# A token, attention and expert tower: value products on whole-number rows, and w1's split and sequence 0's work in other places

## The reference, cut

```python
# token layer: ids in 0..27; counts over a window of three tokens
fused = concat([emb[ids], window_mean(pca_lookup[ids]) @ proj_w + proj_b]) @ fus_w + fus_b
h = ln(fused, 1e-5) * ln_g + ln_b
# attention, 16 heads of 64
y0 = ln(h, 1e-5)
q, k, v = y0 @ Wq + bq, y0 @ Wk + bk, y0 @ Wv + bv
attn = softmax(q k^T / 8)
y = y0 + (attn v) @ Wo + bo
h = h + (ln(y, 1e-3) * gamma + beta)
# experts: 16, two per token, each takes the 64 tokens of a sequence with the greatest route
x = ln(h, 1e-5)
h = h + ln(x + experts(x), 1e-5) * gamma2 + beta2
```

## Time and profile before

| | us |
|---|---|
| median of three runs | 557.83 |
| lowest and highest | 548.49, 558.05 |
| the profiled execution | 547.54 |
| its span, first to last instruction | 545.7 |
| mean granted TensorE clock | 0.993 of full |

### The profile page before, as it was taken

The page is one execution under the profiler, slowest core; times in us unless marked ns, Lnnn a source line. Parts: engine busy times, 40 slices in busy tenths (PEclk is TensorE's granted clock), DMA queues, the critical chain, the costliest instruction groups (busy, mean ns, idle before and its releaser), DMA issues. The chain is left out here.

```text
span 545.7 us, 16180 instructions
## 1 busy us (share of the span) xinstructions
PE 508.7 (93%) x6079; PEld 378.7 (69%) x6079; DVE 439.1 (80%) x986; ACT 363.3 (67%) x766; POOL 379.3 (70%) x508
## 2 busy tenths in 40 slices
PE   5988869999999999999999999788999999999984
PEld 3876557777777777777777786643467767777664
DVE  4797558888888888988888888968777998887675
ACT  2667867878787877878787877517666565556530
POOL 1005567878787878878787878842268798788883
PEclk9998999999999999999999999999999999999998
DMA  7800000000000000000000000000733054261011
GB/s 235 322 4 2 2 2 3 3 3 4 3 2 3 4 2 3 3 3 4 3 2 4 4 2 3 2 0 2 165 82 88 23 131 97 61 145 46 29 40 59
DMA packets 11905, 21.74 MB, mean 40 GB/s; under 512 B 4668, under 2 KB 9780, under 8 KB 10164
## 3 DMA queue, kind: packets, MB, share of 16 engines
q1 hardware_dynamic: 11410, 20.15, 13.5%
q10 hardware_dynamic: 418, 0.55, 0.3%
HBM read 16.24 MB, written 4.33 MB: 38 GB/s over the span
## 5 line engine op out<-in xcount | busy, mean ns | idle before, releaser
L817 POOL TENSOR_TENSOR s_pl<-s_pf,s_ph 128x512 f16<-128x512 f32 x128 | 146.9, 1159 | 5.8 <-ACT s_ph L916 5.8
L1010 DVE TENSOR_REDUCE s_mx<-ps 128x4 f16<-128x512 f32 x128 | 83.8, 677 | 31.8 <-PE ps L1153 31.8
L795 PE MATMUL ps<-s_xt_all,s_w1s 128*128 128x512 f16 x384 | 87.9, 379 | 2.2 <-ACT s_ub L1467 1.6
L1622 PE MATMUL ps<-s_w2s,s_hid 128*128 128x256 f16 x768 | 88.9, 273 | 0.0
L910 ACT ACTIVATE s_pf<-ps 128x512 f32<-128x512 f32 x128 | 76.6, 602 | 15.6 <-PE ps L1166 15.5
L1622 PEld LDWEIGHTS ps<-s_w2s,s_hid 128*128 128x128 f16 x768 | 75.1, 98 | 11.0
L916 ACT ACTIVATE s_ph<-s_pf 128x512 f16<-128x512 f32 x128 | 77.2, 636 | 0.0
L1201 PE MATMUL ps<-s_zh,s_cth 128*128 128x256 f16 x256 | 69.8, 273 | 0.0
L1201 PE MATMUL ps<-s_zh,s_ctl 128*128 128x256 f16 x256 | 69.8, 273 | 0.0
L1201 PE MATMUL ps<-s_zl,s_cth 128*128 128x256 f16 x256 | 69.8, 273 | 0.0
L795 PEld LDWEIGHTS ps<-s_xt_all,s_w1s 128*128 128x128 f16 x384 | 37.3, 98 | 41.4 <-ACT s_ub L1467 2.1
(11 more groups left out here) (233 smaller groups left out, 1211.4 us busy)
## 6 DMA issues: line engine op xcount, KB each, us to landing
s_rep<-picks SPq DMA_DIRECT2D x14, 512.0 KB, 6.2
s_stage<-in_w SPq DMA_DIRECT2D x2, 1024.0 KB, 14.1
out<-s_ot_a SPq DMA_DIRECT2D x16, 128.0 KB, 1.7
out<-s_lg SPq DMA_DIRECT2D x16, 128.0 KB, 1.7
s_stage<-in_wq SPq DMA_DIRECT2D x1, 1024.0 KB, 5.0
s_stage<-in_wk SPq DMA_DIRECT2D x1, 1024.0 KB, 6.6
...
```

The lines of the kernel that those rows point to most:

```text
L795: mm = nc.tensor.matmul(hidden_bank(n)[:], w1s[:, wp, c, j * P:(j + 1) * P], xt_all[:, GB * g:GB * (g + 1), xp, c, :], start=(k == 0), sto ...
L817: nc.gpsimd.tensor_tensor(flat(pl[:, b % 2, 4 * j:4 * j + 4, :]), pf[:, j, :], flat(ph[:, b % 2, 4 * j:4 * j + 4, :]), ALU.subtract).then_ ...
L1010: nc.vector.tensor_reduce(mx[:, b % 2, c:c + 4], A[ab][:].rearrange("p (h k) -> p h k", h=4), AX.X, ALU.max).then_inc(max_done[hf][ab], 1)
L1622: mm = nc.tensor.matmul(zb[b % 4], hid[:, g % 2, hp, j, t * P:(t + 1) * P], w2s[:, wp, j, :], start=False, stop=(j == NJ - 1 and hp == 1))
```

## The change

- **Value products.** The exponentials get a bias per key token (partition), `ln_r`, the logarithm of `r12` times 0.25. So the probabilities hold the factor of `u`, and the value products can use `n` itself, in float16: `nk`, 56 whole numbers, which float16 holds without a low part. Column R2 and R2+1 hold `s1 = v1 * r1` as high and low part, ONE_HI and the next `s12 = s1 * s2`. A head takes two products of 60 columns. ScalarE converts `nb` into `nk` in the first stage, POOL makes the four columns there. The value table gets its R2 and its bias columns twice.
- **The sums** now are two columns: VectorE adds them (`sums`, a reduction of 128x16 to 128x8) and takes the reciprocal of the result from SBUF. The reduction stands where the reciprocal stood; the reciprocal follows the second reduction of maxima (half 0) and y_scaled (half 1). VectorE's waits on itself share one semaphore.
- **The logarithm** is computed once, for all sequences: ScalarE loads the Ln table in step -4, takes Ln of r12, loads Exp in step -3, takes exp(-ln); VectorE corrects it with two small operations (`log_rho`) in step -4 of its order, and the first two exps of sequence 0 wait for it.
- **The maxima** are float32, and `maxima_cols` a float32 transpose.
- **w1**: POOL makes its high part and scales in place before its loop; the low part is made in four pieces of 512 columns in steps -2 and -1, behind probs_lo.
- **Order at the start**: maxima_cols(0) stands ahead of the q products of sequence 1, score_cols(0, 0) ahead of token rows 11 to 13; both halves' first probs_hi of sequence 0 follow its exps directly; token row 13 goes to VectorE.
- `ot_a` lies in zh's place instead of a buffer of its own.

```diff
@@ -40,7 +40,8 @@
 R2, ONE, SHIFT = 2 * V, 2 * V + 1, 2 * V + 2
-UV = ONE + 1
+ONE_HI, UV = R2 + 2, R2 + 4
+RHO_SCALE = 0.25
@@ -118,7 +119,8 @@
 uh, ul = sb("uh", [P, 2, B, UD], F16), sb("ul", [P, 2, B, UD], F16)
-u_top, u_rest = uh[:, 0], ul[:, 0]
+u_top, u_rest, nk = uh[:, 0], ul[:, 0], uh[:, 1]
+r12, ln_r = sb("r12", [P, B]), sb("ln_r", [P, B])
@@ -262,6 +265,23 @@
         nc.gpsimd.memset(nb[:, :, R2:R2 + 1], 1.0).then_inc(cleared, 1)
+        pool.wait_ge(root_step, R1_STEP)
+        nc.gpsimd.tensor_tensor(s1[:], v1[:], r1[:], ALU.mult).then_inc(nk_step, 1)
+        pool.wait_ge(root_step, R2_STEP)
+        pool.wait_ge(v_ok, 1)
+        nc.gpsimd.tensor_tensor(s2[:], v2[:], r2[:], ALU.mult).then_inc(nk_step, 1)
+        pool.wait_ge(nk_step, 2)
+        nc.gpsimd.tensor_tensor(s12[:], s1[:], s2[:], ALU.mult).then_inc(nk_step, 1)
+        def column(n):
+            return nk[:, :, n:n + 1].rearrange("p b o -> p (b o)")
+        pool.wait_ge(nk_step, 3)
+        for n, src in ((R2, s1), (ONE_HI, s12)):
+            nc.gpsimd.tensor_scalar(column(n), src[:], 1.0, 0.0, ALU.mult, ALU.add).then_inc(nk_step, 1)
+        pool.wait_ge(nk_step, 5)
+        for n, src in ((R2, s1), (ONE_HI, s12)):
+            nc.gpsimd.tensor_tensor(column(n + 1), src[:], column(n), ALU.subtract)
@@ -280,6 +300,8 @@
                 .then_inc(nt_ok, 1)
+        act.wait_ge(n_ok, 2)
+        nc.scalar.activation(nk[:, :, 0:2 * V], nb[:, :, 0:2 * V], ACT.Copy)
@@ -302,8 +324,13 @@
             act.wait_ge(qkv_ok, 2 * n + 1)
-            nc.scalar.activation(qkv_t[:, n, :, ONE:ONE + 1], bT[:, n, :].rearrange("p (c o) -> p c o", o=1), ACT.Copy)\
-                .then_inc(qkv_ok, 1)
+            if n < 2:
+                nc.scalar.activation(qkv_t[:, n, :, ONE:ONE + 1], bT[:, n, :].rearrange("p (c o) -> p c o", o=1), ACT.Copy)\
+                    .then_inc(qkv_ok, 1)
+            else:
+                nc.scalar.activation(qkv_t[:, n, :, R2 + 1:R2 + 2], qkv_t[:, n, :, R2:R2 + 1], ACT.Copy).then_inc(qkv_ok, 1)
+                nc.scalar.activation(qkv_t[:, n, :, ONE_HI:UV], bT[:, n, :].rearrange("p (c o) -> p c o", o=1)
+                                     .to_broadcast([P, HD, 2]), ACT.Copy).then_inc(qkv_ok, 1)
@@ -633,7 +660,7 @@
                 pe.wait_ge(wo_step, 2 * HD + 1)
-                pe.wait_ge(qkv_ok, 6)
+                pe.wait_ge(qkv_ok, 7)
@@ -731,9 +758,10 @@
 ph, pl = sb2("ph", [P, 2, H, P], F16), sb2("pl", [P, 2, H, P], F16)
-mx = sb2("mx", [P, 2, H], F16)
+mx = sb2("mx", [P, 2, H])
 mrow = sb2("mrow", [H, 2, P], F16)
-rsum = sb2("rsum", [P, 2, 8])
+rsum, total = sb2("rsum", [P, 2, 8]), sb2("total", [P, 2, 8])
+ln_0, rho_x, rho_t = sb2("ln_0", [P, B]), sb2("rho_x", [P, B]), sb2("rho_t", [P, B])
@@ -853,6 +881,14 @@
                                     ALU.add, ALU.mult).then_inc(x_done, 1)
+        W1_PARTS = {(-2, 0): (0,), (-2, 1): (1,), (-1, 0): (2,), (-1, 1): (3,)}
+        def w1_lo(n):
+            part = slice(512 * n, 512 * n + 512)
+            if n == 0:
+                pool.wait_ge(w_hi, 12)
+            nc.gpsimd.tensor_tensor(both(w1s[:, 1])[:, part], stage2[:, 0, part], both(w1s[:, 0])[:, part], ALU.subtract)
@@ -873,8 +909,9 @@
         pool.wait_ge(w_hi, 10)
-        pool.wait_ge(w1_top, 1)
-        scale_and_lo(both(w1s[:, 0]), both(w1s[:, 1]), stage2[:, 0, :], 10)
+        nc.gpsimd.tensor_scalar(both(w1s[:, 0]), stage2[:, 0, :], W_SCALE, 0.0, ALU.mult, ALU.add).then_inc(w_hi, 1)
+        pool.wait_ge(w_hi, 11)
+        nc.gpsimd.tensor_scalar(stage2[:, 0, :], stage2[:, 0, :], W_SCALE, 0.0, ALU.mult, ALU.add).then_inc(w_hi, 1)
@@ -885,12 +922,16 @@
                 probs_lo(i + 2, 1)
+            for n in W1_PARTS.get((i, 0), ()):
+                w1_lo(n)
...
                 probs_lo(i + 2, 2)
+            for n in W1_PARTS.get((i, 1), ()):
+                w1_lo(n)
@@ -907,7 +948,9 @@
                 act.wait_ge(plo_done[j], b)
-            nc.scalar.activation(pf[:, j, :], ST[j % 2][:], ACT.Exp).then_inc(exp_done[j], 1)
+            if b == 0 and j < 2:
+                act.wait_ge(ln_ok, 4)
+            nc.scalar.activation(pf[:, j, :], ST[j % 2][:], ACT.Exp, bias=ln_r[:, b:b + 1]).then_inc(exp_done[j], 1)
@@ -948,26 +991,32 @@
-        ACT_TOKENS = {(-4, 0): (0, 1, 3, 4, 6, 7), (-3, 0): (9, 10), (-3, 1): (12, 13, 15)}
+        ACT_TOKENS = {(-4, 0): (0, 1), (-4, 2): (3, 4, 6, 7), (-3, 0): (9, 10), (-3, 1): (12, 15)}
...
                 context_hi(i + 1, 0)
-            if has(i + 2):
+            if has(i + 2) and i > -2:
                 probs_hi(i + 2, 1)
+            if i == -3:
+                max_row(0)
...
                 q_hi(i + 4, 0)
-            if has(i + 3):
+            if i == -3:
+                nc.scalar.preload_act_table(ACT.Exp)
+                act.wait_ge(ln_ok, 1)
+                nc.scalar.activation(rho_x[:], ln_0[:], ACT.Exp, scale=-1.0).then_inc(ln_ok, 1)
+            elif has(i + 3):
...
                 q_hi(i + 4, 1)
-            if i == -3:
-                nc.scalar.preload_act_table(ACT.Exp)
...
                 token_rows(n)
-            if i == -3:
-                act.wait_ge(in_w12, 48)
-                nc.scalar.activation(both(w1s[:, 0]), stage2[:, 0, :], ACT.Copy, scale=W_SCALE).then_inc(w1_top, 1)
+            if i == -4:
+                nc.scalar.preload_act_table(ACT.Ln)
+                nc.scalar.activation(ln_0[:], r12[:], ACT.Ln).then_inc(ln_ok, 1)
+            for n in ACT_TOKENS.get((i, 2), ()):
+                token_rows(n)
@@ -985,15 +1034,23 @@
                 exps(i + 3, 1)
+            if i == -3:
+                probs_hi(0, 0)
+                probs_hi(0, 1)
...
                 y_squares(i + 1)
-            if has(i + 3):
+            if has(i + 3) and i > -3:
...
     def _(dve):
+        def step(*what):
+            dve_count[0] += 1
+            steps[what] = dve_count[0]
@@ -1010,13 +1067,26 @@
+        def log_rho():
+            dve.wait_ge(ln_ok, 2)
+            nc.vector.tensor_tensor(rho_t[:], rho_x[:], r12[:], ALU.mult).then_inc(ln_ok, 1)
+            dve.wait_ge(ln_ok, 3)
+            nc.vector.scalar_tensor_tensor(out=ln_r[:], in0=rho_t[:], scalar=float(np.log(RHO_SCALE)) - 1.0, in1=ln_0[:],
+                                           op0=ALU.add, op1=ALU.add).then_inc(ln_ok, 1)
+        def sums(b, hf):
+            dve.wait_ge(pv_ready[hf], b + 1)
+            step("sum", hf)
+            nc.vector.tensor_reduce(total[:, hf], CB[hf][:].rearrange("p (h u) -> p h u", u=UD)[:, :, ONE_HI:UV], AX.X, ALU.add)\
+                .then_inc(dve_step, 1)
         def sum_root(b, hf):
-            dve.wait_ge(pv_ready[hf], b + 1)
-            nc.vector.reciprocal(rsum[:, hf].rearrange("p (h o) -> p h o", o=1),
-                                 CB[hf][:].rearrange("p (h u) -> p h u", u=UD)[:, :, ONE:ONE + 1]).then_inc(rs_done[hf], 1)
+            dve.wait_ge(dve_step, steps["sum", hf])
+            step("root", hf)
+            nc.vector.reciprocal(rsum[:, hf], total[:, hf]).then_inc(dve_step, 1)
...
         def context(b, hf):
-            dve.wait_ge(rs_done[hf], b + 1)
+            dve.wait_ge(dve_step, steps["root", hf])
@@ -1040,10 +1110,11 @@
             dve.wait_ge(h2_done, b + 1)
-            nc.vector.bn_stats(bsx[:, b % 2, :], tok[:, b, :]).then_inc(bsx_done, 1)
+            step("stats", 0)
+            nc.vector.bn_stats(bsx[:, b % 2, :], tok[:, b, :]).then_inc(dve_step, 1)
...
         def x_stats(b):
-            dve.wait_ge(bsx_done, b + 1)
+            dve.wait_ge(dve_step, steps["stats", 0])
@@ -1060,10 +1131,10 @@
                 b = 2 * n + k
-                nc.vector.tensor_scalar(tok[:, b, :], YB[:, k * D:(k + 1) * D], sig[:, b:b + 1], None, ALU.mult)\
-                    .then_inc(tok_done[2], 1)
-
-        DVE_TOKENS = {(-5, 0): (2,), (-5, 1): (5,), (-5, 2): (8,), (-4, 0): (11,), (-4, 1): (14,)}
+                nc.vector.tensor_scalar(tok[:, b, :], ROWS[n % 3][:, k * D:(k + 1) * D], sig[:, b:b + 1], None, ALU.mult)\
+                    .then_inc(tok_done[n % 3], 1)
+        DVE_TOKENS = {(-5, 0): (2,), (-5, 1): (5,), (-5, 2): (8,), (-4, 0): (11,), (-4, 1): (13, 14)}
@@ -1075,10 +1146,14 @@
                 maxima(i + 5, 0, 1)
+            if i == -4:
+                log_rho()
+            if has(i + 3):
+                sums(i + 3, 0)
+            if has(i + 5):
+                maxima(i + 5, 0, 0)
...
                 sum_root(i + 3, 0)
-            if has(i + 5):
-                maxima(i + 5, 0, 0)
@@ -1093,11 +1168,13 @@
             if has(i + 3):
-                sum_root(i + 3, 1)
+                sums(i + 3, 1)
...
                 y_scaled(i + 2)
+            if has(i + 3):
+                sum_root(i + 3, 1)
@@ -1179,9 +1256,9 @@
                     h = 8 * hf + 4 * ab + t
-                    for n, (p, u) in enumerate(((ph, u_top), (ph, u_rest), (pl, u_top))):
-                        mm = nc.tensor.matmul(CB[hf][:, c:c + UV], p[:, b % 2, h, :], u[:, b, 0:UV],
```

(33 more changed lines are left out.)

## The result

| | before | after |
|---|---|---|
| median, 20 executions each, us | 548.42 | 542.56 |
| the profiled execution, us | 547.54 | 541.58 |
| its span, us | 545.7 | 539.7 |
| ratio to before, 95% interval | | 0.9893 (0.9875 to 0.9911) |

The change takes 5.9 us, 1.1%. Forecast were 11.6: the sign holds, half of the gain is missing. First the page of the kernel after, its busy shares.

The account below looks back on a forecast made before the run. PE's issue was taken to bound the attention steps, with the row-statistics chain level with it afterwards. Start -3.2, 29 intervals -9.0 and tail +0.6 made -11.6, so 547.5 became 536 us (forecast 532 to 540, range 529 to 549).

Parts of the forecast that it names:

- The value products: Attention step on PE: 32 products instead of 48, with 60 columns each, save 0.40 us per step.
- The maxima product: Attention step on PE: the float32 transpose takes 0.11 us instead of 0.06, +0.05, making PE's own step 8.52.
- What is late next: Attention step: the row-statistics chain from residual product to normalised rows is level with PE, 8.56 us, 0.31 saved per step.
- the other chain: Second half of a step: late reciprocal delays VectorE's context to 203.32; PE's transposes, reached at 203.40, still find it ready.
- Rival (a): Attention steps: VectorE's order or the row chain costs 0.2 to 0.3 more; period 8.7 to 8.8, 542 us; chance 0.26.
- The start: Start of the second stage: first value product 2.9 us earlier, sequence 2's q products at 74.3 instead of 77.52, -3.2.
- w1's part: Start, POOL: w1 work no longer stands ahead, so both low halves are made by 67.3 instead of 72.1.
- the logarithm's sum: Start: the chain over Ln, Exp and VectorE's token row, reduction and two logarithm operations ends at 63.3; then exps(0) begins.
- the clock: Start, PE: a clock fall in the gaps was named as making the forecast wrong; no time was given to it.
- The bias: ScalarE's exponentials: a bias from a column costs nothing, at most 0.16 us per step on an engine with room.
- The tail: After the last maxima product: fewer products bring nothing, the late reciprocal costs 0.2 in each of three steps, +0.6 us.
- The first stage's copies: First stage, ScalarE: copying 1792 counts, about 1.7 us, fits into a 4.17 us wait for PE and costs nothing.

Follow-up runs that it names:

- the first experiment: The changed kernel with the second half's reciprocal put ahead of y_scaled instead of behind it: 536.83 us, ratio to before 0.9803.
- fifth experiment: The kernel before with the change of w1 alone (high part and scaling ahead of POOL's loop, low part in four pieces): 545.24 us beside 548.28, ratio 0.9932.
- the eighth experiment: The changed kernel with the reciprocal ahead of y_scaled and float16 maxima with their old product: 537.61 us, ratio to before 0.9782.

## Why the prediction was half right

- **The value products:** right, 0.40 forecast, 0.401 measured per step (0.736 + 0.642 less 0.536 + 0.441).
- **The maxima product** ("+0.05 per step"): the product itself is right, the step is not. Float32 saves 0.09 ahead of it, so PE's own step is 8.43 and not 8.52. The forecast priced the instruction and not its distance to the one before.
- **What is late next** ("this chain is level with PE", 8.56): this is the step that failed. The normalised rows never set the step: their transposes show no wait, and PE runs at 8.433 past them in the first experiment. What set it was the other chain, which the forecast called "just in time" with 0.08 to spare. PE came 0.09 earlier than reckoned, by the maxima product; and behind the context stood `ctl`, which was named but not followed to PE's output products: 0.11 of the 0.19 are there. Forecast 9.0 us for the 29 intervals, measured 6.0, and 11.5 with the reciprocal early. Rival (a) had this mechanism with 0.2 to 0.3 over PE's own step. Its 542 us is what came, but in part by luck: with shorter steps than it had (8.63, it had 8.7 to 8.8) and a start that gave less.
- **The start** (-3.2, measured -0.4 at the third maxima product). w1's part is right in the main (2.5, fifth experiment), and so is the logarithm's sum: reckoned at 63.3, it came at 64.08 with the stage 0.9 later. What the sum left out is the clock behind PE's gaps: the forecast only named its fall as what would make it wrong, and so it went. The first value product was forecast 69.3 - 46.7 = 22.6 behind the first q product and came at 24.39. The fall's 1.6, read from the eighth experiment's profile, taken off leaves an estimated 22.8; with the logarithm early and no fall it is 22.73. The stage's later begin is 0.9 more: 0.37 of it are POOL's columns, which had been costed at nothing since POOL was free, where VectorE paid; the rest is within what the begin moves from profile to profile.
- **The bias** ("nothing", at most 0.16 per step): in time right, in size wrong, 92 ns each or 0.37 per step; the rows compared both had a column as an operand, so their difference couldn't show its price.
- **The tail** (+0.6): +0.4 in the changed kernel.
- **The first stage's copies** on ScalarE: right, hidden.
